# Layer norm terms made per group of four blocks inside the stages, instead of for all blocks between them

## What is computed

```python
A = tanh(x @ W.T + W_b + b); s = A @ V.T + V_b              # a score per token
w = softmax(s over windows of 4 tokens, stride 2)           # 127 windows
h = (sum of w * x in a window) @ P.T + P_b                  # tokens become 127 patches
h = h + attention(layernorm(h)) @ w_proj.T + b_proj         # 8 heads, query and key parts mixed in 3 versions
n = layernorm(h)
h = h + n + expert(n)                                       # 4 experts, the one with the largest logit, gelu between
layernorm(x) = (x - mean) / sqrt(var + 1e-5)
```

## Time and profile before

| what | value |
|---|---|
| median of 3 runs | 2064.79 us (2064.35 to 2069.66) |
| the profiled execution | 2065.83 us, span 2063.9 us |
| PE busy | 1911.3 us, 93% |
| DVE busy | 1478.8 us, 72% |
| ACT busy | 1410.4 us, 68% |
| POOL busy | 1162.1 us, 56% |
| granted TensorE clock, mean | 0.973 |

### The profile page before, as it was taken

One profiled execution on the slowest core, in us unless ns is written; L12 is line 12 of the kernel. 1 busy time (PEld: TensorE's weight loads), 2 busy tenths in 40 slices (PEclk: granted clock), 3 DMA queues, 4 the chain that ended last, 5 costly groups with the idle time before them and its releaser, 6 DMA issues. The chain is left out here.

```text
span 2063.9 us, 60351 instructions
## 1 busy us (share of the span) xinstructions
PE 1911.3 (93%) x20800; PEld 1179.2 (57%) x20800; DVE 1478.8 (72%) x3636; ACT 1410.4 (68%) x2978; POOL 1162.1 (56%) x2198
## 2 busy tenths in 40 slices
PE   3999999993999999999999999999991899999998
PEld 3999999980444444444444444444441566666666
DVE  4555555553899999999999999999981455555554
ACT  1333333330889899899898998998982666666665
POOL 1111111127677777777777777777756565565561
PEclk9999999995999999999999999999996899999999
DMA  4444444421444444444444444444440332322322
GB/s 138 127 114 117 121 122 122 122 62 29 80 89 89 88 90 88 90 88 90 90 86 90 90 90 89 89 88 90 87 80 13 57 64 62 71 62 63 71 63 52
DMA packets 512122, 176.03 MB, mean 85 GB/s; under 512 B 452169, under 2 KB 511308, under 8 KB 512076
## 3 DMA queue, kind: packets, MB, share of 16 engines
q1 hardware_dynamic: 512075, 175.43, 38.7%
HBM read 53.79 MB, written 12.48 MB: 32 GB/s over the span
## 5 line engine op out<-in xcount | busy, mean ns | idle before, releaser
L692 DVE TENSOR_REDUCE tops<-p_maxa 128x6 f32<-128x762 f32 x512 | 483.0, 943 | 61.9 <-PE p_maxa L534 60.7
L605 PE MATMUL p_o<-probs,vn 127*32 127x256 f32 x6144 | 410.7, 385 | 0.2 <-DVE att L720 0.2
L530 PE MATMUL p_s<-qm,kt 32*128 32x256 f16 x3072 | 399.1, 275 | 1.3 <-ACT probs L649 0.4
L646 ACT ACTIVATE probs<-p_s 128x512 f32<-128x512 f32 x512 | 305.4, 596 | 108.4 <-PE p_s L530 95.6
L694 DVE TENSOR_REDUCE tops<-p_maxb 128x4 f32<-128x508 f32 x512 | 346.4, 676 | 0.0
L652 ACT ACTIVATE probs<-p_s 128x512 f32<-128x512 f32 x512 | 309.4, 604 | 0.0
L649 ACT ACTIVATE probs<-p_s 128x512 f32<-128x512 f32 x512 | 304.9, 596 | 0.3 <-PE p_s L530 0.2
L966 DVE TENSOR_TENSOR gel_lo<-gel,gel_hi 128x512 f16<-128x512 f32 x192 | 147.4, 768 | 215.7 <-ACT gel_hi L956 214.4
L534 PE MATMUL p_maxa<-kt,qt 24*128 24x256 f16 (+1 forms) x2048 | 284.1, 250 | 16.0 <-DMA kt<-qk 8.5
L360 POOL TENSOR_TENSOR diag<-ident,weight 128x256 f32<-128x256 f32 x128 | 78.9, 617 | 369.2 <-DVE band L339 328.3
L530 PEld LDWEIGHTS p_s<-qm,kt 32*128 32x128 f16 x3072 | 134.7, 91 | 182.9 <-issue 168.6
(11 more groups left out here) (186 smaller groups left out, 4522.3 us busy)
## 6 DMA issues: line engine op xcount, KB each, us to landing
xn<-in_xn SPq DMA_DIRECT2D x32, 768.0 KB, 6.3
xt_a<-in_xt SPq DMA_DIRECT2D x32, 512.0 KB, 4.4
out<-out_sb SPq DMA_DIRECT2D x32, 336.0 KB, 2.7
xt_b<-in_xt SPq DMA_DIRECT2D x32, 256.0 KB, 5.2
xt<-hx SPq DMA_TRANSPOSE x128, 2.3
kt<-qk SPq DMA_TRANSPOSE x128, 2.7
qt<-qk SPq DMA_TRANSPOSE x128, 2.4
qm<-qk SPq DMA_TRANSPOSE x128, 2.7
```

Of the source, the lines that this page charges most:

```text
L530: return nc.tensor.matmul(o, kt[full(j), r, kind, g, :], qm[full(j), r % 2, versions, g, :], start=True, stop=True, skip_group_check=True)
L605: last = nc.tensor.matmul(p_o[32 * j:32 * j + 32, blocks, :], vn[0:NP, r, src:src + 32], probs[0:NP, r % 2, QUAD * g + j, kind * 256:(kind ...
L646: nc.scalar.activation(probs[:, r % 2, h + 1, 0:512], p_s[1][:, :, :].rearrange("p x n -> p (x n)"), ACT.Exp, scale=SCALE).then_inc(act_e1 ...
L692: nc.vector.tensor_reduce(top[:, q, pair, 4:10], p_ma[:, 0:6, 0:NP], AX.X, ALU.max, negate=True).then_inc(dve_ma[u], 1)
```

## The change

- In the first stage VectorE's `terms` makes mean, variance and scales of the group whose moments are complete, in steps at k = 1, 2 and 3 of a round, between the band and the moments of the next block. POOL makes the power of four columns at k = 2, behind the diagonal. The moments go to a small tile with two halves. The last group's terms take a round at the end of the stage.
- The stage `norm_terms` is removed, and both calls of it.
- In attention the moments are taken out of VectorE's round. The three minima become a reduction over pairs and one operation over two thirds of the slots.
- In the last stage VectorE takes the moments of group i + 4, one block behind each of the residuals 2 to 5 (`moments`), then makes the variance (`variance`). POOL makes the power of group i + 3 at the start of a round, ahead of its four blocks (`body`, the old body is now `four`). VectorE makes the scales of group i + 3 between the choice and the second residual (`scales`); ScalarE's first normalisation of a round waits for them. The rounds begin at i = -4 instead of -2.

```diff
-        dve_stats = sem("dve_stats")
+        stats = sb("stats", [128, 2, G, 6])
+        mean, gap, var, root = (sb(x, [128, G]) for x in ("mean", "gap", "var", "root"))
+        dve_stats, dve_norm, pool_root = sem("dve_stats"), sem("dve_norm"), sem("pool_root")
...
+            def terms(i, par, step):
+                g = i - 3
+                if not within(g, NG):
+                    return
+                st = stats[:, 1 - par]
+                if step == 1:
+                    dve.wait_ge(dve_stats, seen((i - 2) * G))
+                    if not isinstance(i, int) or i > 3:
+                        dve.wait_ge(dve_norm, seen((i - 3) * 4))
+                    nc.vector.tensor_tensor(mean[:, :], st[:, :, 1], st[:, :, 4], ALU.add)
+                    nc.vector.tensor_tensor(gap[:, :], st[:, :, 1], st[:, :, 4], ALU.subtract)
+                    nc.vector.tensor_tensor(var[:, :], st[:, :, 2], st[:, :, 5], ALU.add).then_inc(dve_norm, 1)
+                elif step == 2:
+                    dve.wait_ge(dve_norm, seen((i - 2) * 4 - 3))
+                    nc.vector.tensor_tensor(gap[:, :], gap[:, :], gap[:, :], ALU.mult)
+                    nc.vector.tensor_scalar(var[:, :], var[:, :], 1.0 / C, EPS, ALU.mult, ALU.add).then_inc(dve_norm, 1)
+                    dve.wait_ge(dve_norm, seen((i - 2) * 4 - 2))
+                    nc.vector.scalar_tensor_tensor(out=var[:, :], in0=gap[:, :], scalar=0.25, in1=var[:, :],
+                                                   op0=ALU.mult, op1=ALU.add).then_inc(dve_norm, 1)
+                elif step == 3:
+                    dve.wait_ge(pool_root, seen(i - 2))
+                    nc.vector.tensor_copy(t.rstd[:, bass.ds(g * G, G)], root[:, :])
+                    nc.vector.scalar_tensor_tensor(out=t.shift[:, bass.ds(g * G, G)], in0=mean[:, :], scalar=-0.5, in1=root[:, :],
+                                                   op0=ALU.mult, op1=ALU.mult).then_inc(dve_norm, 1)
+
             def body(i, par, half):
...
                         last.then_inc(dve_band, 1)
+                    terms(i, par, k)
                     u = n - 2 * G - 1
                     if within(u, NB):
+                        q, kk = (par, k - 1) if k else (1 - par, G - 1)
                         dve.wait_ge(act_h, seen(u + 1))
-                        nc.vector.bn_stats(t.stats[:, bass.ds(u * 6, 6)], t.h[:, bass.ds(u * C, C)]).then_inc(dve_stats, 1)
+                        nc.vector.bn_stats(stats[:, q, kk, :], t.h[:, bass.ds(u * C, C)]).then_inc(dve_stats, 1)
             loop(dve, body)
 
...
                         nc.gpsimd.tensor_tensor(diag[:, 1 - two, :, :], t.ident[:, :].unsqueeze(1).broadcast_to([128, 2, 128]),
                                                 weight[:, up, kk, 0:2].unsqueeze(2).broadcast_to([128, 2, 128]), ALU.mult)\
                             .then_inc(pool_diag, 1)
+                    if k == 2 and within(i - 3, NG):
+                        pool.wait_ge(dve_norm, seen((i - 2) * 4 - 1))
+                        nc.gpsimd.tensor_tensor(root[:, :], var[:, :], t.half[:, :], ALU.pow).then_inc(pool_root, 1)
             loop(pool, body)
-
-def norm_terms(nc, t, NB, name):
...
-        @block.vector
-        def _(dve):
-
-            nc.vector.tensor_tensor(mean[:, :], st[:, :, 1], st[:, :, 4], ALU.add)
-            nc.vector.tensor_tensor(gap[:, :], st[:, :, 1], st[:, :, 4], ALU.subtract)
-            nc.vector.tensor_tensor(var[:, :], st[:, :, 2], st[:, :, 5], ALU.add).then_inc(step, 1)
-            dve.wait_ge(step, 1)
-            nc.vector.tensor_tensor(sq[:, :], gap[:, :], gap[:, :], ALU.mult)
-            nc.vector.tensor_scalar(var[:, :], var[:, :], 1.0 / C, EPS, ALU.mult, ALU.add).then_inc(step, 1)
-            dve.wait_ge(step, 2)
-            nc.vector.scalar_tensor_tensor(out=var[:, :], in0=sq[:, :], scalar=0.25, in1=var[:, :],
-                                           op0=ALU.mult, op1=ALU.add).then_inc(var_made, 1)
-            dve.wait_ge(root_made, 1)
-            nc.vector.scalar_tensor_tensor(out=t.shift[:, 0:NB], in0=mean[:, :], scalar=-0.5, in1=t.rstd[:, 0:NB],
-                                           op0=ALU.mult, op1=ALU.mult)
-
-        @block.gpsimd
-        def _(pool):
-            pool.wait_ge(var_made, 1)
-            nc.gpsimd.tensor_tensor(t.rstd[:, 0:NB], var[:, :], t.half[:, 0:NB], ALU.pow).then_inc(root_made, 1)
...
             def body(i, r):
                 maxima(i, r, 0)
-                if within(i - 3, NB):
-                    dve.wait_ge(dve_h, seen(i - 2))
-                    nc.vector.bn_stats(t.stats[:, bass.ds((i - 3) * 6, 6)], t.h[:, bass.ds((i - 3) * C, C)])
 
                 maxima(i, r, 1)
                 if within(i + 1, NB):
@@ -705,10 +703,10 @@
                     got = top[:, (r + 1) % 2]
                     four = got[:, :, 0:8].rearrange("p a (e k) -> p a e k", e=2)
                     fifth = got[:, :, 8:10]
-                    low = [slots((r + 1) % 2, 256 * x, HEADS)[:, :, 24].rearrange("p (a e) -> p a e", e=2) for x in range(3)]
-                    nc.vector.tensor_tensor(low[0], four[:, :, :, 0], four[:, :, :, 1], ALU.min)
-                    nc.vector.tensor_tensor(low[1], four[:, :, :, 2], fifth, ALU.min)
-                    nc.vector.tensor_tensor(low[2], four[:, :, :, 3], fifth, ALU.min).then_inc(dve_min, 1)
+                    low = slots((r + 1) % 2, 0, NQ)[:, :, 24].rearrange("p (x a e) -> p x a e", x=3, e=2)
+                    nc.vector.tensor_reduce(low[:, 0], four[:, :, :, 0:2], AX.X, ALU.min)
+                    nc.vector.tensor_tensor(low[:, 1:3], four[:, :, :, 2:4].rearrange("p a e k -> p k a e"),
+                                            fifth.unsqueeze(1).broadcast_to([128, 2, QUAD, 2]), ALU.min).then_inc(dve_min, 1)
...
+        stats = sb("f_stats", [128, G, 6])
+        mean, gap, var, root = (sb("f_" + x, [128, G]) for x in ("mean", "gap", "var", "root"))
+        rstd, shift = sb("f_rstd", [128, 2, G]), sb("f_shift", [128, 2, G])
...
+        dve_stats, dve_norm, pool_root = sem("f_dve_stats"), sem("f_dve_norm"), sem("f_pool_root")
...
-            for i in range(-2, 3):
+            for i in range(-4, 3):
                 body(i, i % U, (i - 1) // 2)
...
-            def norm(i, k):
+            def norm(i, r, k):
                 n = (i + 2) * G + k
                 if within(i + 2, NG):
+                    if k == 0:
+                        act.wait_ge(dve_norm, seen((i + 3) * 4))
                     act.wait_ge(pool_x, seen(n - 1))
                     nc.scalar.activation(hn[:, k % 2, :], t.h[:, bass.ds(n * C, C)], ACT.Identity,
-                                         scale=t.rstd[:, bass.ds(n, 1)], bias=t.shift[:, bass.ds(n, 1)]).then_inc(act_ln, 1)
+                                         scale=rstd[:, r % 2, k:k + 1], bias=shift[:, r % 2, k:k + 1]).then_inc(act_ln, 1)
...
                     if c < G:
-                        norm(i, c)
+                        norm(i, r, c)
...
+            def moments(i, r, k):
+                if within(i + 4, NG):
+                    n = (i + 4) * G + k
+                    nc.vector.bn_stats(stats[:, k, :], t.h[:, bass.ds(n * C, C)]).then_inc(dve_stats, 1)
+
+            def variance(i):
+                if within(i + 4, NG):
+                    dve.wait_ge(dve_stats, seen((i + 5) * G))
+                    nc.vector.tensor_tensor(mean[:, :], stats[:, :, 1], stats[:, :, 4], ALU.add)
+                    nc.vector.tensor_tensor(gap[:, :], stats[:, :, 1], stats[:, :, 4], ALU.subtract)
+                    nc.vector.tensor_tensor(var[:, :], stats[:, :, 2], stats[:, :, 5], ALU.add).then_inc(dve_norm, 1)
+                    dve.wait_ge(dve_norm, seen((i + 4) * 4 + 1))
+                    nc.vector.tensor_tensor(gap[:, :], gap[:, :], gap[:, :], ALU.mult)
+                    nc.vector.tensor_scalar(var[:, :], var[:, :], 1.0 / C, EPS, ALU.mult, ALU.add).then_inc(dve_norm, 1)
+                    dve.wait_ge(dve_norm, seen((i + 4) * 4 + 2))
+                    nc.vector.scalar_tensor_tensor(out=var[:, :], in0=gap[:, :], scalar=0.25, in1=var[:, :],
+                                                   op0=ALU.mult, op1=ALU.add).then_inc(dve_norm, 1)
+
+            def scales(i, r):
+                if within(i + 3, NG):
+                    dve.wait_ge(pool_root, seen(i + 4))
+                    if within(i + 1, NG):
+                        dve.wait_ge(act_ln, seen((i + 2) * G))
+                    nc.vector.tensor_copy(rstd[:, (r + 1) % 2, :], root[:, :])
+                    nc.vector.scalar_tensor_tensor(out=shift[:, (r + 1) % 2, :], in0=mean[:, :], scalar=-0.5, in1=root[:, :],
+                                                   op0=ALU.mult, op1=ALU.mult).then_inc(dve_norm, 1)
+
             def body(i, r, half):
                 low(i, 0)
                 choose(i, r)
+                scales(i, r)
                 low(i, 1)
                 for k in range(G):
                     output(i, r, half, k)
```

(13 more changed lines are left out.)

## The result

The changed kernel takes 2104.61 us (median of 4 runs, 2093.02 to 2106.95) where the kernel before takes 2064.88 beside it: a ratio of **1.0186**, interval 1.0142 to 1.0229; one more run, outside this median, took 2112.49. It is slower, and the prediction had said faster. Of the lines, L970 is now the residual, L979 to L996 the choice, L1032 and L1033 the scales, L1006 the output, L911 the first down matmul.

What follows compares the result with a forecast made beforehand. TensorE's queue was taken to set each stage's end, VectorE mattering only where TensorE waits for it. From the profiled 2065.8 us, -21.1 - 17.5 - 2 + 17.1 gave 2042.3, or 2041 against the median; range 2015 to 2135.

Steps and rivals of the forecast that it cites:

- first rival: Last stage: VectorE's choice lets several POOL operations pass each round, 2.5 us x 30 = 75 us more, 2116 us; chance 0.32.
- First and second boundary: Where stages meet, a short chain of layer norm terms replaces the standstill: -21.1 us before attention, -17.5 us after it.
- First stage: Eight small VectorE operations and one POOL power per round of four blocks hide behind a full TensorE: zero.
- Attention: VectorE loses the moments and one of three minima, but the loop through TensorE stays: -2 us.
- Last stage: Per round, added waits, scales and a possible POOL hold of the second residual lengthen VectorE's chain 0.57 us: +17 us in 30.
- Starved choice: Last stage: POOL running without a gap under VectorE's choice delays it, 75 us on top, 2116 us; chance 0.32.
- Power with a large fixed part: POOL's small power takes 2 us instead of 0.83, in 30 rounds and 3 in the chains: 2080 us; chance 0.08.

Runs made afterwards that it cites:

- the run with late scales: The changed kernel with the two scale operations moved from ahead of the second residual to behind the four outputs; 2048.94 us, 0.9905 of the kernel before.

## Why the prediction was wrong

The forecast was 2041 us and faster; the kernel takes 2104.61 and is slower. That the range of 2015 to 2135 still holds the result is owed to the room left for the first rival, whose mechanism is not what happened. By parts:

- **First and second boundary**: -21.1 and -17.5 us, as predicted. That they agree to the tenth is luck in part: the power took 1.02 us and not 0.83, twice in the second chain, and small operations priced a little too high made up for it (four moments 1.07 us for 1.2, a variance 0.8 for 0.9).
- **First stage**: zero predicted, 0.6 us measured.
- **Attention**: -2 predicted, +1.8 measured, within the runs' spread. The reading held: VectorE lost 35 us of work there and waited longer instead, 28 us of it ahead of the maxima over the first tile (72.1 us idle where the earlier trace rows has 44.2), and the stage got no shorter:

```profile
L693 DVE TENSOR_REDUCE tops<-p_maxa 128x6 f32<-128x762 f32 x482 | 457.2, 949 | 72.1 <-PE p_maxa L535 53.0
```

- **Last stage**: this step failed. "Sum 0.57, in 30 rounds +17 us". Measured: +1.38 us of chain in nearly every round, more than twice the 0.57, and rounds longer by 2.3 us on average. By its terms: the first residual -0.29, where +0.17 stood, as it does not wait for the power; the choice +0.44, where nothing stood; the scales 0.80, where 0.20 and 0.05 stood; the second residual +0.43, where 0.15 stood. The prices were taken one by one, each against the POOL that the trace of before shows. That POOL has a gap just where they fall, from 1824.50 to 1824.77 (before, timeline of POOL):

```profile
1823.95 0.55 POOL L1037 TENSOR_TENSOR f_hx<-f_hn,f_hx 128x192 f16<-128x192 f32 x1
1824.77 0.93 POOL L1033 TENSOR_TENSOR f_hx<-f_hn,f_one 128x192 f16<-128x192 f32 x1 [0.28 <-ACT f_hn L935]
```

  In it the second residual began, at 1824.66, and was free for its 0.69 us. The prediction said that POOL would have no gap there any more, and then took the scales at the gap's price and the residual at a third of a hold. The upper bound of 1.0 us was too low for the same reason.
- **The clock**: missing altogether, a term put at nothing without a word. The prediction counted TensorE's wait as time lost once. At 1.2 us of wait, as it forecast, that would have been right (the run with late scales, with up to 1.4 us, stays at 1.00); at 2.0 it adds 1.65 us (17.1 against 15.44) in 16 rounds of 28, 26 us: about all by which the span grew.
- **Starved choice**, the rival that came out on this side: it gave 2116 us, near the result, by another mechanism. An operation that lets several of POOL's pass is seen in the first choice alone (L983, 2.44 us at 1564.66). In the steady rounds each held operation lost at most one POOL operation, 0.63 us being the longest of a four-column one. The rule of the Trainium skill, SBUF — State Buffer, section "SBUF: two separate sides", that the shared ports are locked for a whole instruction, fits these rows. It was the count of held operations, not the length of a hold, that was too low: in the round shown seven are stretched from the choice to the second residual, where the prediction had priced the two residuals. Where the Trainium skill says there that a GpSimd operation that starts first holds the pair for the whole instruction, the 28 residuals that ran at full speed under a power of 1.02 us differ.
- **Power with a large fixed part**: 1.02 us, of which by two sizes (4 columns 1.02, 11 columns 2.18) some 0.36 is fixed. That is under the 1.6 from which it would have decided.

## What to carry to other kernels

Price an operation that is added to a shared-port engine's critical chain against the neighbour as it will stand after the change, and all of them together: here the same two operations cost 0.15 us where POOL leaves a gap and 0.75 where its blocks run 2.5 us later, and the late blocks by themselves cost 0.2 us or 0.7 by a shift of three tenths of a microsecond. When a change lengthens a wait of TensorE that comes back in every round, ask whether its clock will hold: here waits of 1.3 us cost only their own length, and those of 2.0 cost 1.65 us more in 16 rounds of 25. Work that is moved out of a boundary into a loop belongs into the loop's gaps, of both engines: there the same change gives 1.7 to 2.0% instead of costing 1.9, and 2.7% with the outputs moved ahead as well, a step that the kernel before might also gain by (not run).

## What was not expected of the hardware

- TensorE's clock falls to half behind a wait of 2.0 us that comes once in a round, though not in every round: in the changed kernel 9 of 25 keep the full clock, three in a row each time. What decides it between them stays open.
- A power on POOL doesn't hold VectorE's residual, an operation with two operands from SBUF (0.68 to 0.69 us in 28 rounds of two runs), while block operations of half its length do (up to 1.1 us).
- VectorE's copy and its operation with scalars (L1032, 0.16 to 0.63 us; L996, 0.17 to 0.41) are held by POOL like the two-operand ones, though each has one operand.
